# Graph attention on one core: the order of each graph's blocks, and which PSUM bank a graph's turn uses

## The reference

```python
q = (x @ Wq.T); k = (x @ Wk.T); v = (x @ Wv.T + bv)      # 12 heads of 32
a = einsum('bnhd,bmhd->bhnm', q, k) * SCALE + adj[:, None]
pad_mask = all(a == 0, axis=-1)
a = nan_to_num(softmax(where(pad_mask[..., None], -inf, a), axis=-1))
o = einsum('bhnm,bmhd->bnhd', a, v).reshape(B, N, HIDDEN)
x = layernorm(x + o @ Wo.T + bo)
```

## Time and profile before

| | us |
|---|---|
| median of 3 runs | 1276.09 (1274.07 to 1276.71) |
| the profiled execution: its own time | 1274.01 |
| its span, first to last instruction | 1272.2 |
| PE busy | 1225.0 |
| DVE busy | 1039.1 |
| ACT busy | 1022.4 |
| POOL busy | 859.3 |

### The profile page before, as it was taken

One profiled execution on the slowest core, in us unless ns is written; L12 is line 12 of the kernel. 1 busy time (PEld: TensorE's weight loads), 2 busy tenths in 40 slices (PEclk: granted clock), 3 DMA queues, 4 the chain that ended last, 5 costly groups with the idle time before them and its releaser, 6 DMA issues.

```text
span 1272.2 us, 34265 instructions
## 1 busy us (share of the span) xinstructions
PE 1225.0 (96%) x11742; PEld 1053.9 (83%) x11742; DVE 1039.1 (82%) x5094; ACT 1022.4 (80%) x4007; POOL 859.3 (68%) x775
## 2 busy tenths in 40 slices
PE   8999999999999999999999999999999999999986
PEld 7888888888888888888888888888888888888875
DVE  5778888888888788888888887888888888878886
ACT  6877888878788778888887887788887878877874
POOL 1766767667667667676676676676766766766675
PEclk9999999999999999999999999999999999999998
DMA  6022112222122221122221222211222202222100
GB/s 228 22 70 84 61 46 84 78 70 78 34 79 78 70 84 59 47 84 78 70 78 34 79 78 70 84 63 43 84 78 70 78 32 80 79 70 84 47 26 32
DMA packets 58895, 88.85 MB, mean 70 GB/s; under 512 B 3680, under 2 KB 54624, under 8 KB 58720
## 3 DMA queue, kind: packets, MB, share of 16 engines
q1 hardware_dynamic: 58720, 86.65, 20.2%
HBM read 61.47 MB, written 25.17 MB: 68 GB/s over the span
## 4 chain that ended last, share of the span: by engine, by line
PE 70%; DVE 24%; issue 3%; POOL 2%; ACT 1%; DMA 0%; DVEq 0%; POOLq 0%; SPq 0%
PE turn_bank L211 16%; PE turn_bank L213 16%; PE turn_bank L212 16%; PE pT_bank L248 9%; PE score_bank L235 7%; PE turn_bank L260 6%; DVE neg_a L511 6%; DVE out_sb L575 3%; DVE xT_lo L487 3%; DVE stats L560 3%; DVE y_sb L555 3%; DVE neg_sum L523 2%; POOL inv_std L661 1%; DVE v_sb L501 1%; DVE mean_var L564 1%
## 5 line engine op out<-in xcount | busy, mean ns | idle before, releaser
L396 ACT ACTIVATE probs<-neg_a,neg_max 128x128 f32<-128x128 f32 x1536 | 596.6, 398 | 1.9 <-DVE neg_max L511 1.9
L654 POOL TENSOR_TENSOR probs<-probs,row_scale 128x768 f32<-128x768 f32 x256 | 376.6, 1471 | 191.7 <-DVE row_scale L539 191.7
L647 POOL TENSOR_TENSOR fold<-neg_a 128x384 f32<-128x384 f32 x256 | 271.8, 1062 | 168.6 <-DVE neg_max L511 168.6
L511 DVE CUSTOM_DVE_ANT_0 neg_a<-score_bank,adj_sb 128x128 f32<-128x128 f32 x1536 | 333.2, 285 | 0.2
L403 ACT ACTIVATE pT<-pT_bank 128x384 f32<-128x384 f32 x512 | 220.8, 485 | 103.4 <-PE pT_bank L248 103.3
L396 ACT ACTIVATION_READ_ACCUMULATOR probs<-neg_a,neg_max 128x1 f32 x1536 | 302.8, 197 | 0.0
L211 PE MATMUL turn_bank<-xT_hi,w_hi 128*128 128x512 f32 x576 | 241.0, 418 | 29.4 <-DVE xT_lo L487 27.6
L213 PE MATMUL turn_bank<-xT_hi,w_lo 128*128 128x512 f32 x576 | 227.7, 395 | 0.0
L212 PE MATMUL turn_bank<-xT_lo,w_hi 128*128 128x512 f32 x576 | 227.6, 395 | 0.0
L248 PE MATMUL pT_bank<-ident,probs 128*128 128x128 f32 x1536 | 217.3, 278 | 0.3 <-ACT pT L403 0.3
L389 ACT ACTIVATE qkT<-turn_bank 128x512 f32<-128x512 f32 x192 | 113.7, 592 | 100.2 <-PE turn_bank L213 96.8
(11 more groups left out here) (38 smaller groups left out, 2021.9 us busy)
## 6 DMA issues: line engine op xcount, KB each, us to landing
xT_raw<-xT_dram SPq DMA_DIRECT2D x32, 768.0 KB, 6.3
x_sb<-x_dram SPq DMA_DIRECT2D x32, 768.0 KB, 5.2
out_dram<-out_sb SPq DMA_DIRECT2D x128, 192.0 KB, 1.9
adj_sb<-adj_dram SPq DMA_DIRECT2D x32, 256.0 KB, 3.0
w_raw<-wq_t_dram SPq DMA_DIRECT2D x1, 576.0 KB, 5.7
w_raw<-wk_t_dram SPq DMA_DIRECT2D x1, 576.0 KB, 6.8
w_raw<-wv_t_dram SPq DMA_DIRECT2D x1, 576.0 KB, 7.8
w_raw<-wo_t_dram SPq DMA_DIRECT2D x1, 576.0 KB, 8.4
```

The lines of the kernel that those rows point to most:

```text
L396: last = nc.scalar.activation(probs[b % 2][:, u, :], neg_a[b % 2][:, u, :], ACT.Exp, bias=neg_max[b % 2][:, u:u + 1], scale=-1.0, accum_ou ...
L511: last = nc.vector.tensor_tensor_reduce(out=neg_a[b % 2][:, u, :], in0=score_bank[trio][:, c * N:(c + 1) * N], in1=adj_sb[p][:, b, :], sca ...
L647: nc.gpsimd.tensor_tensor(fold[:, u, :], neg_a[b % 2][:, u, 0:N // 2], neg_a[b % 2][:, u, N // 2:N], ALU.add).then_inc(fold_done, 1)
L654: nc.gpsimd.tensor_tensor(probs[b % 2][:, u, :], probs[b % 2][:, u, :], row_scale[:, u].unsqueeze(2).broadcast_to([P, HALF, N]), ALU.mult) ...
```

## The change

The helpers are the same and each does what it did, the same number of times. What moves is their order on each engine, the banks, and one wait or another with them:

- `ATTEND_BANK` goes from (0, 1, 1, 0) to (0, 0, 1, 1). With it `project_v` and `project_qk` get other banks.
- PE: a slot is now scores, attend, transposes pair 0, projection, transposes pair 1, projection, `project_out`, where it was attend, scores, pair 0, projection, `project_out`, pair 1, projection. The extra `project_qk` still ends slots 0 and 2.
- ACT: the exponentials of trios 1 to 3 move behind the copies; the input split of chunk 1 goes to slot 0 and of chunk 2 to slot 1; `keep_qk` of blocks 3 and 0 goes to the end of slots 0 and 2.
- DVE: bias trios 0 and 1 go ahead of `keep_oT_lo`; the layer norm's first four steps come after the second `keep_v`, and `mask_half(1)` comes before `normalise` instead of after it; `keep_xT_lo` of chunks 0 and 1 goes to slot 1.
- POOL: `add_bo` goes ahead of the first `scale_half`.
- SP: the transposed input of a quad is asked for one quad earlier.

```diff
-ATTEND_BANK = (0, 1, 1, 0)
+ATTEND_BANK = (0, 0, 1, 1)
...
@@ sync
+                    if b == 3 and q + 3 < QUADS:
+                        sp.wait_ge(xT_lo_done, CHUNKS * q + 3 * CHUNKS)
+                        load_xT(q + 3)
...
@@ tensor, slots 2 and 3
-                pe.wait_ge(y_read, QUAD * q + 3)
-                attend(j, p, 2)
                 if has_next:
                     pe.wait_ge(qk_done, QK * q + 2 * QK)
                     pe.wait_ge(neg_a_done, 16 * q + 16)
                     scores(*nxt, 0)
+                attend(j, p, 2)
                 transpose_probs(j, p, 3, 0)
+                pe.wait_ge(y_read, QUAD * q + 3)
                 if has_next:
                     project_v(*nxt, 0, 0)
-                project_out(j, p, 2)
                 transpose_probs(j, p, 3, 1)
                 if has_next:
                     pe.wait_ge(v_done, QUAD * q + QUAD + 1)
                     project_v(*nxt, 1, 0)
-
+                project_out(j, p, 2)
                 if has_after:
+                    pe.wait_ge(v_done, QUAD * q + QUAD + 2)
                     pe.wait_ge(xT_lo_done, CHUNKS * q + 3 * CHUNKS)
-                    pe.wait_ge(y_read, QUAD * q + 4)
-                    project_qk(*aft, 0, 1)
-                if has_next:
-                    pe.wait_ge(v_done, QUAD * q + QUAD + 2)
-                attend(j, p, 3)
+                    project_qk(*aft, 0, 0)
...
@@ scalar
                 if more2:
                     exp_trio(*later(j, p, b, 2), 0)
-                    exp_trio(*later(j, p, b, 2), 1)
                 if b == 1 and has_next:
                     keep_qk(*nxt, 4, turn)
...
                 if more2:
-                    exp_trio(*later(j, p, b, 2), 3)
-                if b == 0 and has_after:
-                    act.wait_ge(v_psum, QUAD * (2 * j + p) + QUAD)
-                    keep_xT_hi(*aft, 0)
+                    exp_trio(*later(j, p, b, 2), 1)
                 if b == 1 and has_next:
                     keep_qk(*nxt, 5, turn)
...
@@ vector
+                if more2:
+                    bias_trio(*later(j, p, b, 2), 0)
+                    bias_trio(*later(j, p, b, 2), 1)
                 keep_oT_lo(j, p, b)
...
-                residual(j, p, b)
-                statistics(j, p, b)
-                mean_variance(j, p, b)
-                add_eps(j, p, b)
                 if b == 2 and has_after:
-                    keep_xT_lo(*aft, 1)
                     keep_xT_lo(*aft, 2)
                 if b == 0:
                     keep_v(j, p, 3, turn)
                 if b == 2 and has_next:
                     keep_v(*nxt, 1, turn)
+                residual(j, p, b)
+                statistics(j, p, b)
+                mean_variance(j, p, b)
+                add_eps(j, p, b)
+                if more2:
+                    mask_half(*later(j, p, b, 2), 1)
                 normalise(j, p, b)
-                if more2:
-                    mask_half(*later(j, p, b, 2), 1)
...
@@ gpsimd
+                if b + 1 < QUAD or has_next:
+                    add_bo(*later(j, p, b, 1))
+                if more2:
                     scale_half(*later(j, p, b, 2), 0)
                 inverse_std(j, p, b)
-                if b + 1 < QUAD or has_next:
-                    add_bo(*later(j, p, b, 1))
```

More of the change, by code:

```diff
@@ L275, in quad @@
                 nxt, aft = ahead(j, p, 1), ahead(j, p, 2)
-                pe.wait_ge(y_read, QUAD * q + 1)
-                attend(j, p, 0)
                 pe.wait_ge(neg_a_done, 16 * q + 8)
                 scores(j, p, 2)
-                transpose_probs(j, p, 1, 0)
                 if has_next:
                     pe.wait_ge(qk_done, QK * q + QK + 3)
+                else:
+                    pe.wait_ge(v_done, QUAD * q + 2)
+                attend(j, p, 0)
+                transpose_probs(j, p, 1, 0)
+                pe.wait_ge(y_read, QUAD * q + 1)
                 project_v(j, p, 2, 1)
-                project_out(j, p, 0)
                 transpose_probs(j, p, 1, 1)
@@ L288, in quad @@
                 project_v(j, p, 3, 1)
+                project_out(j, p, 0)
+                pe.wait_ge(v_done, QUAD * q + 4)
                 if has_next:
-                    pe.wait_ge(y_read, QUAD * q + 2)
-                    project_qk(*nxt, 3, 0)
-                pe.wait_ge(v_done, QUAD * q + 4)
-                attend(j, p, 1)
+                    project_qk(*nxt, 3, 1)
                 pe.wait_ge(neg_a_done, 16 * q + 12)
                 scores(j, p, 3)
+                pe.wait_ge(y_read, QUAD * q + 2)
+                attend(j, p, 1)
                 transpose_probs(j, p, 2, 0)
@@ L299, in quad @@
                     pe.wait_ge(qk_done, QK * q + QK + 4)
-                    project_qk(*nxt, 4, 0)
-                project_out(j, p, 1)
+                    project_qk(*nxt, 4, 1)
                 transpose_probs(j, p, 2, 1)
@@ L304, in quad @@
                     pe.wait_ge(qk_done, QK * q + QK + 5)
-                    project_qk(*nxt, 5, 0)
-                pe.wait_ge(y_read, QUAD * q + 3)
-                attend(j, p, 2)
+                    project_qk(*nxt, 5, 1)
+                project_out(j, p, 1)
                 if has_next:
@@ L331, in quad @@
                     scores(*nxt, 1)
+                pe.wait_ge(y_read, QUAD * q + 4)
+                attend(j, p, 3)
+                if has_next:
                     transpose_probs(*nxt, 0, 0)
@@ L334, in quad @@
                     pe.wait_ge(qk_done, QK * q + 2 * QK + 1)
-                    project_qk(*aft, 1, 1)
-                project_out(j, p, 3)
+                    project_qk(*aft, 1, 0)
                 if has_next:
@@ L340, in quad @@
                     pe.wait_ge(qk_done, QK * q + 2 * QK + 2)
-                    project_qk(*aft, 2, 1)
+                    project_qk(*aft, 2, 0)
+                project_out(j, p, 3)
             pe.wait_ge(ident_steps, 2)
@@ L417, in graph @@
                 more2 = b + 2 < QUAD or has_next
-                if b == 1 and has_next:
-                    keep_qk(*nxt, 3, turn)
-                if b == 3 and has_after:
-                    keep_qk(*aft, 0, turn)
                 keep_oT_hi(j, p, b)
@@ L432, in graph @@
                     keep_qk(*aft, 1, turn)
-                if b == 2 and has_after:
-                    keep_xT_hi(*aft, 2)
-                if more2:
-                    exp_trio(*later(j, p, b, 2), 2)
                 if more:
@@ L449, in graph @@
                 if b == 1 and has_after:
+                    keep_xT_hi(*aft, 2)
+                if more2:
+                    exp_trio(*later(j, p, b, 2), 2)
+                    exp_trio(*later(j, p, b, 2), 3)
+                if b == 0 and has_after:
+                    act.wait_ge(v_psum, QUAD * (2 * j + p) + QUAD)
+                    keep_xT_hi(*aft, 0)
                     keep_xT_hi(*aft, 1)
+                if b == 0 and has_next:
+                    keep_qk(*nxt, 3, turn)
+                if b == 2 and has_after:
+                    keep_qk(*aft, 0, turn)
             def quad(j, p, has_next, has_after):
@@ L581, in graph @@
                 more2 = b + 2 < QUAD or has_next
+                if more2:
+                    bias_trio(*later(j, p, b, 2), 0)
+                    bias_trio(*later(j, p, b, 2), 1)
                 keep_oT_lo(j, p, b)
                 if more2:
-                    for trio in range(4):
-                        bias_trio(*later(j, p, b, 2), trio)
-                if b == 1 and has_after:
-                    keep_xT_lo(*aft, 0)
+                    bias_trio(*later(j, p, b, 2), 2)
+                    bias_trio(*later(j, p, b, 2), 3)
                 if b == 0:
```

10 lines of the change are left out of this document (6 added, 4 removed).

## The result

The changed kernel takes **1384.8 us** (median of 4 runs, 1383.2 to 1386.5) against 1275.1 for the kernel before on the same chip (1274.1 to 1276.7): 1.0859 times as long, 95% interval 1.0840 to 1.0879. The profiled execution has a span of 1383.2 us at a mean granted clock of 0.994, so the span grew by 111.0 us.

A forecast was written before the change was run, and what follows sets the result against it. PE, busy 96% of the span, was taken to bound the kernel. Against the profiled 1274.0 us, -32 + 120 + 16 - 1 = +103 gave 1377, stated as 1378 for the median; range 1340 to 1440.

The forecast's parts named there:

- The stall of slots 0 and 2: PE's second value projection waits for DVE's copy of the first: 2.0 us, 60 times, +120 us.
- The forecast chain: DVE's work from the residual to the first value copy, T being the scores' start; PE resumes T+6.54 instead of T+4.53.
- The query/key projection of slots 1 and 3: The second projection into one bank waits for ACT's copy: 0.27 us, 60 times, +16 us.
- the sign that I gave for it: In the profile after, PE would wait for `qkT` some 60 times, about 0.3 us each.
- The input stall: PE's wait for the last low input chunk at slot 2's end goes: 1.08 us, 30 times, -32 us.
- The scaled probabilities: Second transposes wait for POOL's scaling, hidden inside the slot 0 and 2 stall; 0.3 to 0.5 us if exposed.
- The ends: First attend's wait goes, -0.8 us; last quad's waits shuffle, bounded at 2 us either way, taken as 0.
- B: Rival: `normalise` on DVE loses the shared port to POOL's second scaling, adding 82 us: 1460 us; chance 0.07.
- C: Rival: PE's clock falls to half in the slot 0 and 2 stalls, adding 90 to 114 us: 1470 to 1490; chance 0.13.
- D: Rival: not slower, layer norm clears DVE early, slots 0 and 2 stall 0.27 us: 1274 us; chance 0.05.
- E: Rival: tighter DVE bias, copies or mask half make the slot 0 and 2 stall 1.0 to 1.5 us: 1317 to 1347; chance 0.10.

The follow-up runs named there:

- kernel with early input: Kernel before, with all high input chunks in slot 0, low chunk 0 in slot 0, low chunks 1 and 2 in slot 1, transfer a quad earlier: 1239.1 us.
- The first input experiment: Kernel before, with only the change's input part: transfer a quad earlier, low chunks 0 and 1 in slot 1, chunk 2 in slot 2: 1273.2 us.

## Why the prediction was right, and where it was off

The forecast was 1378; the time is 1384.8, inside the range, and by the mechanism forecast. The distance of 7 us flatters the sum a little. From profiled execution to profiled execution I had +103, and it is +111; the 1 us that I added because the median lay above the profiled execution before took one off by luck, since after the change it does not (1384.8 against 1385.0).

**The stall of slots 0 and 2** (forecast 2.0 us). An undisturbed slot is 9.93 us, the changed kernel's 11.95: 2.02. The forecast chain had the residual at T+0.18, `normalise` at T+2.53, the low part of the attention output at T+4.19, the copy at T+5.92 and PE at T+6.54; the trace has 0.17, 2.51, 4.17, 5.90 and 6.51. That this chain is the path is shown by the run with an instruction more inside it and the one with it outside, and by the removal of 81 us when the copies are moved out of it. That the place of `project_out` on PE is not the cause by itself is shown by the two runs that undo it.

**The query/key projection of slots 1 and 3** (forecast 0.27 us). 9.21 against 8.94: 0.27. Its 16 us were right, but the sign that I gave for it was not: no 60 waits of PE for `qkT` of about 0.3 us are in the list, only one of 0.7. In the timeline the block of transposes ends at 709.68 and the projection starts at 709.72, so almost no idle time is left to show, and the 0.27 us are the last transpose running out.

**The input stall** (forecast -1.08 us, 30 times). The slot with the stall is 11.10 us in the kernel before and 9.93 in the kernel with early input: 1.17, and that kernel is 35 us faster in its medians. The term was right in kind and 3 us small. That it goes in the new order rested on a count ("over 1 us" to spare); in the trace the last low chunk ends at 701.25 and the projection starts at 702.18, 0.93 us later. The first input experiment shows how easily another wait takes its place.

**The scaled probabilities** (0.3 to 0.5 if they were exposed). 0.25 us of idle time at pair 1, inside the 2.02, and in the kernel with copies and chunk moved, where DVE is on time, still there and part of the 0.74 us by which its slot exceeds 9.93.

**The ends were the mis-sized term** (forecast -1, with 2 us either way). The scores of slot 0 of the first quad and of slot 2 of the last quad but one, in the timelines of PE before, and then after:

```profile
37.36 0.84 PE L235 MATMUL score_bank<-qkT 32*128 32x128 f32 x20
...
1222.74 0.95 PE L235 MATMUL score_bank<-qkT 32*128 32x128 f32 x24
```

```profile
35.66 0.95 PE L237 MATMUL score_bank<-qkT 32*128 32x128 f32 x24
...
1326.98 0.95 PE L237 MATMUL score_bank<-qkT 32*128 32x128 f32 x24
```

Between them lie 61 pairs of slots: 1185.4 us before, 1291.3 after, +105.9, where I had 60 pairs and +104. The start gained 1.7. The tail, from there to the end of the span, took 49.46 us before and 56.22 after: +6.8. Three rows of the tail after:

```profile
1341.18 1.38 PE L250 MATMUL pT_bank<-ident,probs 128*128 128x128 f32 x6 [1.82 <-POOL probs L660]
...
1359.35 0.87 PE L250 MATMUL pT_bank<-ident,probs 128*128 128x128 f32 x6 [1.82 <-POOL probs L660]
...
1364.84 1.16 PE L250 MATMUL pT_bank<-ident,probs 128*128 128x128 f32 x6 [2.26 <-POOL probs L660]
```

In the last slots the projection between the two transposes is missing, so pair 1 meets the scaled probabilities directly, and these now come behind the layer norm and the second mask half; the waits for DVE's copy go on as well (1.26 us at 1351.65). The clock has a small part in it at most: it fell in the tail of both kernels, with means of 0.86 before and 0.84 after, so that by estimate (49.5 x 0.14 against 56.2 x 0.16) no more than 2 of the 6.8 us come from it. "The last quad's waits shuffle" is the term that was mis-sized: I had bounded it without walking through it. Also, the first slot of all is 12.45 us long and stalls 2.5 us, not 0.3: no layer norm is ahead of it, but the last mask half of the prologue is, and DVE waits in that for ACT's exponentials until 38.68, T+3.0. 105.9 - 1.7 + 6.8 = 111.0, the whole growth of the span.

**The rivals.** B did not happen: `normalise` took 0.48 us in every slot, since it started 0.09 us after the row scale and POOL 0.25 after it, as argued, and POOL's second scaling took 1.65 us (at 716.28) instead of 1.47; the run with one instruction between them shows what the other order costs. The Trainium skill, SBUF — State Buffer, section "SBUF: two separate sides", says that a DVE instruction with two SBUF inputs is locked out in the same way by a GpSimd instruction that reads SBUF; the 0.94 us of the six-element `row_scale` beside `add_bo` agrees. C did not happen in the steady part (one window from 100 to 1341 us reads 1.00), but it was nearer than its chance of 0.13 said: two runs that lengthened the idle time to about 1.95 and 2.3 us a slot saw the clock fall in over half of these slots. The sum of the idle time does not decide it alone. With `project_out` back in slots 0 and 2 PE idled 0.65 and 1.74 us in a slot 2, 2.39 in all, but the waits ended at 716.72 and 722.51 and not some 2.1 us apart as in those two runs; there the clock read 1.00 from 100 to 1396 us. What kept it up at 1.5 us in the changed kernel is not settled beyond these points. The price of C rested on a wrong reading: I had the clock back at about 1241.8 and so 3.8 us at half speed, but it read 0.50 from 1238 to 1241, 0.76 from 1241.0 to 1241.5 and 1.00 from there on the earlier trace rows, about 3.4 us. That prices a fall at up to 1.7 us instead of 1.9, and the 1.58 us measured lie within it. D and E had no support in the chain, which had no hole.

## What to carry to other kernels

Where a PSUM bank is written twice in a row, write down for both projections what the reading engine has in its order ahead of the copy, from the moment at which its last wait ends; the longer of the two chains is the price, and it is paid in every slot because nothing in it waits for the late engine. Moving one engine's order alone, forward or back, gives a new wait behind another engine: after each move, ask which queue is late next (here the second copy, then an input chunk, then nothing). Walk through the ends with the same care as the steady state, since blocks that cover a wait there are missing.

## What the runs showed of the hardware that I had not expected

- A DVE instruction of six elements is held like a large one, until POOL's instruction is over: `row_scale` took 0.94 us beside `add_bo`, against 0.17 alone, and ended 0.02 us behind it; a low chunk took 1.25 us beside a fold, against 0.69 alone.
- Idle times of 0.69 and 1.26 us, neither long in itself, brought PE's granted clock down in some slots (0.66 in the 5 us behind them) and left it at 1.00 in others; 0.25 and 1.26 never brought it down in the steady part of the changed kernel. 0.65 and 1.74 us, further apart, left it at 1.00 as well. One instruction of 0.55 us more on DVE, 128 times, cost from 0 to 172 us, depending on which of its neighbours it pushed.
